# GNN layer on one core: node stage in pairs of blocks, and the output weights scaled by GpSimd

## The reference, cut to what matters

```
h   = relu(layernorm(x))                       # per node
l   = (h @ W_l1) * a                           # per node: the table
w   = relu(edge_basis @ W_fc1) @ W_fc2         # per edge, 192 weights
m   = products of w, l[src] and edge_attr      # per edge
s   = segment_sum(m, dst)                      # per node
out = x + h @ W_si + 0.5 * (s @ W_l2) * a      # per node
```

## Time and profile before

| | us |
|---|---|
| three runs, median (lowest to highest) | 2140.87 (2136.94 to 2141.41) |
| the profiled execution | 2140.02 |
| its span in the profile | 2138.2 |
| busy: PE, DVE, ACT, POOL | 2017.2, 1701.0, 345.4, 1570.7 |
| first gather starts | 89.44 |
| last gather starts | 2118.7 |

### The profile page before, as it was taken

How to read it: one execution, slowest core, us unless ns; L and a number is a source line. 1 busy time by engine, 2 the same in 40 slices (tenths; PEclk the granted TensorE clock), 3 DMA queues, 4 the chain that set the end, 5 groups by cost and what they waited for, 6 DMA issues and landing times.

```text
span 2138.2 us, 42050 instructions
## 1 busy us (share of the span) xinstructions
PE 2017.2 (94%) x11466; PEld 1594.1 (75%) x11466; DVE 1701.0 (80%) x4661; ACT 345.4 (16%) x657; POOL 1570.7 (73%) x1631
## 2 busy tenths in 40 slices
PE   4899999999999999999999999999999999999998
PEld 4677777777777777777777777777777777777776
DVE  7578888878887788788888887888887788888886
ACT  3411111111111111111111111111111111111111
POOL 5277777777777777777777777777777777777775
PEclk9789999999998999999999999999999899998998
DMA  4222322232232233222233232223222222232223
GB/s 123 79 72 69 73 72 70 70 73 71 71 72 69 70 72 72 70 72 71 71 102 73 70 72 71 72 70 73 72 70 72 70 70 71 71 72 70 72 71 91
DMA packets 159932, 158.29 MB, mean 74 GB/s; under 512 B 86882, under 2 KB 131846, under 8 KB 159914
## 3 DMA queue, kind: packets, MB, share of 16 engines
q0 software_dynamic: 77376, 132.16, 24.9%
q1 hardware_dynamic: 81400, 24.49, 5.1%
q10 hardware_dynamic: 1138, 1.43, 0.2%
HBM read 149.90 MB, written 8.03 MB: 74 GB/s over the span
## 4 chain that ended last, share of the span: by engine, by line
POOL 35%; issue 26%; DMA 18%; DVE 15%; PE 4%; POOLq 1%; ACT 0%; DVEq 0%; ACTq 0%; SPq 0%
POOL y L353 35%; DMA y<-table,idx 17%; DVE hot L648 5%; DVE msg L624 5%; DVE dot L618 3%; PE ps_s L850 1%; DVE wself L552 1%; PE ps_s L852 1%; PE ps_w L822 1%; DVE dots L614 1%; DMA table<-y 0%; PE ps_h L815 0%; POOLq L361 0%; PE ps_w L785 0%; DVE stats L508 0%
## 5 line engine op out<-in xcount | busy, mean ns | idle before, releaser
L353 POOL DMA_INDIRECT y<-table,idx x1612 | 1540.0, 955 | 544.1 <-issue 499.4
L822 PEld LDWEIGHTS ps_w<-w_fc,hr 100*128 100x128 f32 x3224 | 539.5, 198 | 331.7 <-issue 331.7
L822 PE MATMUL ps_w<-w_fc,hr 100*128 100x192 f32 x3224 | 663.2, 351 | 0.0
L850 PE MATMUL ps_s<-hot,msg 128*128 128x128 f32 x3224 | 486.3, 298 | 62.2 <-DVE msg L634 61.5
L850 PEld LDWEIGHTS ps_s<-hot,msg 128*128 128x128 f32 x3224 | 437.3, 207 | 107.9 <-DVE msg L634 106.0
L447 ACT ACTIVATE hr<-ps_h 100x512 f32<-100x512 f32 x403 | 240.6, 597 | 1676.8 <-PE ps_h L815 1676.8
L815 PE MATMUL ps_h<-rad,w_fc 10*100 10x512 f32 x806 | 464.3, 657 | 4.9 <-DMA rad<-in_radial 4.9
L614 DVE TENSOR_TENSOR dots<-y,attr_sb 128x384 f32<-128x384 f32 x403 | 225.3, 559 | 280.0 <-DMA y<-table,idx 279.5
L852 PE MATMUL ps_s<-hot,msg 128*128 128x64 f32 x3224 | 432.0, 281 | 0.0
L852 PEld LDWEIGHTS ps_s<-hot,msg 128*128 128x128 f32 x3224 | 423.3, 205 | 0.0
L676 DVE TENSOR_TENSOR acc<-acc,ps_s 64x32 f32 (+1 forms) x1612 | 324.8, 201 | 72.1 <-PE ps_s L852 32.2
(11 more groups left out here) (79 smaller groups left out, 520.4 us busy)
## 6 DMA issues: line engine op xcount, KB each, us to landing
y<-table,idx POOLq DMA_INDIRECT x1612
rad<-in_radial SPq DMA_DIRECT2D x202, 40.0 KB
xres<-in_x SPq DMA_DIRECT2D x7, 560.0 KB, 4.0
table<-y SPq DMA_DIRECT2D x6, 560.0 KB, 3.2
out<-xres SPq DMA_DIRECT2D x6, 560.0 KB, 4.7
idx<-in_src SPq DMA_DIRECT2D x202, 4.0 KB
attr_sb<-in_attr SPq DMA_DIRECT2D x202, 16.0 KB
dst_i<-in_dst ACTq DMA_DIRECT2D x1, 808.0 KB, 6.0
```

The source lines that it names most:

```text
L353: nc.gpsimd.indirect_dma_start(out=y[:, j, t, :], out_offset=None, in_=table, in_offset=bass.IndirectOffsetOnAxis(ap=idx[:, j // HALF, col ...
L822: ins = nc.tensor.matmul(ps_w[:, s, t, 0:NW], hr[:, s, t * P:(t + 1) * P], w_fc2[:, :], start=True, stop=True)
L850: nc.tensor.matmul(ps_s[:, s, 0:4 * W], msg[:, s, t, 0:P], hot[:, s, t, 1:V, :], start=(t == 0), stop=(t == T - 1))
```

## The change

The blocks of a chunk are grouped in four units: blocks 0-1, 2-3, 4-5 and block 6. Per unit there is one copy on ScalarE (512 columns for a pair), one take on VectorE, and one semaphore step each for turning, product and take. The take becomes a `tensor_tensor` of PSUM columns with the attribute broadcast along them, where it was a `tensor_scalar` with a per-partition scalar. The six in-place weight scalings leave VectorE's queue; GpSimd does them ahead of its memset, each waiting for the one before. The side work of VectorE is attached to units 2 of chunk 0 and 0 to 3 of chunk 1. `hid_t` has two places of two blocks each.

```diff
@@ -18,8 +18,9 @@
-LAST_STORES = [(0, 4), (4, CHUNK)]
-TURNED = [0, 1, 0, 1, 0, 1, 2]
+UNITS = [(0, 2), (2, 4), (4, 6), (6, CHUNK)]
+NU = len(UNITS)
+assert NU % 2 == 0
...
@@ -102,7 +103,7 @@
-        hid_t = sb("hid_t", [P, max(TURNED) + 1, 2 * P])
+        hid_t = sb("hid_t", [P, 2, 2, 2 * P])
...
@@ -242,8 +244,8 @@
-            for n, (lo, hi) in enumerate(LAST_STORES):
-                store_table(CHUNKS - 1, CHUNKS - 1 + n, (CHUNKS - 1) % 2, lo, hi)
+            for n, units in enumerate((2, NU)):
+                store_table(CHUNKS - 1, CHUNKS - 1 + n, (CHUNKS - 1) % 2, UNITS[units - 2][0], UNITS[units - 1][1], units)
...
@@ -338,6 +340,12 @@
+            pool.wait_ge(ld_w, 80)
+            for n, (part, scale) in enumerate(((wself[:, 0:MUL0], MUL0 ** -0.5), (wself[:, MUL0:P], MUL1 ** -0.5),
+                                               (wselfz[:, :], MUL1 ** -0.5), (w_out[:, 0:3, :], K_SUM),
+                                               (w_out[0:3 * MUL1, 3, :], K_SUM), (w_out[3 * MUL1:P, 3, :], K_SUM * K_DOT))):
+                nc.gpsimd.tensor_scalar(part, part, float(scale), None, ALU.mult).then_inc(w_end_scaled, 1)
+                pool.wait_ge(w_end_scaled, n + 1)
...
@@ -415,26 +423,30 @@
-                def move(b):
-                    act.wait_ge(tr_done, c * CHUNK + b + 1)
-                    nc.scalar.activation(hid_t[:, TURNED[b], :], ps_h[:, b % 2, 0:2 * P], ACT.Copy).then_inc(hidt_done, 1)
-                for b in range(CHUNK):
-                    if b < CHUNK - 1:
-                        normalize(c * CHUNK + b + 1, b + 1)
+                def move(u):
+                    lo, hi = UNITS[u]
+                    act.wait_ge(tr_done, c * NU + u + 1)
+                    nc.scalar.activation(hid_t[:, u % 2, 0:hi - lo, :], ps_h[:, u % 2, 0:(hi - lo) * 2 * P].rearrange("p (b k) -> p b k", k=2 * P),
+                                         ACT.Copy).then_inc(hidt_done, 1)
+                for u in range(NU):
+                    if u < NU - 1:
+                        for b in range(*UNITS[u + 1]):
+                            normalize(c * CHUNK + b, b)
                     elif not last:
                         act.wait_ge(norm_done, c + 2)
-                        normalize(c * CHUNK + CHUNK, 0)
-                    move(b)
-                    if b == 3 and not last:
+                        for b in range(*UNITS[0]):
+                            normalize((c + 1) * CHUNK + b, b)
+                    move(u)
+                    if u == 1 and not last:
                         deviation(c + 1)
             nc.scalar.activation(early[:, :], eps[:, :], ACT.Sqrt)
             deviation(0)
             act.wait_ge(norm_done, 1)
-            normalize(0, 0)
+            for b in range(*UNITS[0]):
+                normalize(b, b)
...
@@ -522,13 +534,15 @@
-            def take(c, parity, b, first):
-                if not first and b == 0:
+            def take(c, parity, u, first):
+                if not first and u == 0:
                     dve.wait_ge(table_out, c * 16 - 16)
-                dve.wait_ge(node_mm, c * CHUNK + b + 1)
-                nc.vector.tensor_scalar(l_st[:, parity, b, :], ps_w[:, b % 2, 0, 0:C],
-                                        a_sb[:, bass.ds(c * CHUNK + b, 1)], None, ALU.mult).then_inc(l_done, 1)
+                lo, hi = UNITS[u]
+                dve.wait_ge(node_mm, c * NU + u + 1)
+                nc.vector.tensor_tensor(l_st[:, parity, lo:hi, :], ps_w[:, u % 2, 0:hi - lo, 0:C],
+                                        a_sb[:, bass.ds(c * CHUNK + lo, hi - lo)].unsqueeze(2).to_broadcast([P, hi - lo, C]),
+                                        ALU.mult).then_inc(l_done, 1)
...
@@ -543,13 +557,6 @@
-            def scale_more():
-                dve.wait_ge(ld_w, 80)
-                for part, scale in ((wself[:, 0:MUL0], MUL0 ** -0.5), (wself[:, MUL0:P], MUL1 ** -0.5),
-                                    (wselfz[:, :], MUL1 ** -0.5), (w_out[0:3 * MUL1, 3, :], K_SUM),
-                                    (w_out[:, 0:3, :], K_SUM), (w_out[3 * MUL1:P, 3, :], K_SUM * K_DOT)):
-                    nc.vector.tensor_scalar(part, part, float(scale), None, ALU.mult).then_inc(w_scaled, 1)
...
@@ -580,23 +587,22 @@
-                for b in range(CHUNK):
+                for u in range(NU):
                     if not last:
-                        if b == 0:
+                        if u == 0:
                             statistics(c + 1, range(0, 4))
-                        if b == 1:
+                        if u == 1:
                             statistics(c + 1, range(4, CHUNK))
-                        if b == 2:
                             aggregate(c + 1)
-                        if b == 4:
+                        if u == 2:
                             normalizers(c + 1)
-                    take(c, parity, b, first)
-                    if b in between:
-                        between[b]()
-            chunk(0, 0, True, False, {3: distances, 5: scale_more})
-            chunk(1, 1, True, False, {0: farthest, 2: nearest, 3: lowest, 5: outside})
+                    take(c, parity, u, first)
+                    if u in between:
+                        between[u]()
+            chunk(0, 0, True, False, {2: distances})
+            chunk(1, 1, True, False, {0: farthest, 1: nearest, 2: lowest, 3: outside})
...
@@ -765,35 +771,37 @@
-            def had_bank(b):
-                return b - 2 if b >= 2 else -1 - b
-            def turn(c, b, first=False):
-                pe.wait_ge(hid_done, c * CHUNK + b + 1)
+            def turn(c, u, first=False):
+                lo, hi = UNITS[u]
+                pe.wait_ge(hid_done, c * CHUNK + hi)
                 if not first:
-                    pe.wait_ge(hidt_done, c * CHUNK + had_bank(b) + 1)
-                nc.tensor.transpose(ps_h[:, b % 2, 0:P], hid[:, b, 0:P], ident[:, :])
-                nc.tensor.transpose(ps_h[:, b % 2, P:2 * P], hid[:, b, C - P:C], ident[:, :]).then_inc(tr_done, 1)
+                    pe.wait_ge(hidt_done, c * NU + u - 1)
+                for n, b in enumerate(range(lo, hi)):
+                    nc.tensor.transpose(ps_h[:, u % 2, n * 2 * P:n * 2 * P + P], hid[:, b, 0:P], ident[:, :])
+                    ins = nc.tensor.transpose(ps_h[:, u % 2, n * 2 * P + P:(n + 1) * 2 * P], hid[:, b, C - P:C], ident[:, :])
+                ins.then_inc(tr_done, 1)
             def chunk(c, first, last):
-                def linear(b):
-                    pe.wait_ge(hidt_done, c * CHUNK + b + 1)
-                    if b >= 2 or not first:
-                        pe.wait_ge(l_done, c * CHUNK + had_bank(b) + 1)
-                    nc.tensor.matmul(ps_w[:, b % 2, 0, 0:P], hid_t[:, TURNED[b], 0:P], wl[:, :], start=True, stop=True)
-                    nc.tensor.matmul(ps_w[:, b % 2, 0, P:C], hid_t[:, TURNED[b], P:2 * P], wlz[:, :], start=True, stop=True).then_inc(node_mm, 1)
-                for b in range(CHUNK):
-                    if b < CHUNK - 1:
-                        turn(c, b + 1, first and b == 0)
+                def linear(u):
+                    lo, hi = UNITS[u]
+                    pe.wait_ge(hidt_done, c * NU + u + 1)
+                    if u >= 2 or not first:
+                        pe.wait_ge(l_done, c * NU + u - 1)
+                    for n in range(hi - lo):
+                        nc.tensor.matmul(ps_w[:, u % 2, n, 0:P], hid_t[:, u % 2, n, 0:P], wl[:, :], start=True, stop=True)
+                        ins = nc.tensor.matmul(ps_w[:, u % 2, n, P:C], hid_t[:, u % 2, n, P:2 * P], wlz[:, :], start=True, stop=True)
+                    ins.then_inc(node_mm, 1)
+                for u in range(NU):
+                    if u < NU - 1:
+                        turn(c, u + 1, first and u == 0)
                     elif not last:
                         turn(c + 1, 0)
-                    if first and b == 0:
+                    if first and u == 0:
                         pe.wait_ge(w_scaled, 3)
-                    linear(b)
-                    if first and b == 1:
+                    linear(u)
+                    if first and u == 0:
...
@@ -806,7 +814,7 @@
-            pe.wait_ge(w_scaled, 9)
+            pe.wait_ge(w_end_scaled, 6)
```

More of the change, by code:

```diff
@@ L158, in gnn_layer @@
         w_scaled = sem("w_scaled")
+        w_end_scaled = sem("w_end_scaled")
         bn_done = sem("bn_done")
@@ L229, in _, with store_table @@
                 load_x(c, False)
-            def store_table(c, stores, parity, lo, hi):
-                sp.wait_ge(l_done, c * CHUNK + hi)
+            def store_table(c, stores, parity, lo, hi, units=NU):
+                sp.wait_ge(l_done, c * NU + units)
                 sp.sem_inc(sp_passed, 1)
@@ L449, in move_block @@
             def move_block(b, n, bank):
-                act.wait_ge(tr_done, b + (BLOCKS + 1))
-                nc.scalar.activation(hid_t[:, n, :], ps_h[:, bank, 0:2 * P], ACT.Copy).then_inc(hidt_done, 1)
```

(10 more changed lines are left out.)

## The result

The changed kernel's runs have a median of 2134.31 us (2129.95 to 2139.31, 7 runs), the kernel before 2139.85 (2134.9 to 2143.29, 7 runs). The ratio is 0.9975, 95% interval 0.9964 to 0.9986: about 5 us faster, where 11.5 were forecast, and 2134.31 is above the range's end of 2133. The profiled execution took 2139.31 us, the longest of the seven, with a span of 2137.5. So the document compares the stages inside it, and its total only through the seven runs.

What follows compares the result with a forecast made beforehand. GpSimd's gathers were taken to bound the kernel, so only the first gather's start counted. Chunk 2's VectorE queue starting at 38.7 instead of 49.21, plus 1.0 ahead, gave 11.5 us: 2140.02 to 2128.5 us, range 2126 to 2132 (2121 to 2133 with the unheld case).

Steps and rivals of the forecast that it cites:

- What bounds the kernel: Whole run: gathers keep their own pace of 1.26 us, so only an earlier first gather shortens the total.
- Part 1: VectorE's weight scalings in chunk 0: moving them off ends a hold by GpSimd's clear, 15.4 us, plus 0.8 us.
- Part 3: VectorE's `outside` step (L577, L578): its tensor_scalar moves forward into GpSimd's clear and is held 6.2 us, from 32.3 to 38.5.
- rival A: VectorE's small tensor_scalar is not held by the clear: 16.9 us won, 2123.1 us; chance 0.25.
- Rival B: VectorE's new tensor_tensor take in chunk 0 is held by the clear: 6.1 us slower, 2146.1 us; chance 0.04.
- One sign of being wrong: VectorE inside GpSimd's clear: the forecast is wrong if a take there lasts over 1 us.
- Part 2: GpSimd ahead of its clear: the six scalings take 2.6 us, so the clear runs from 17.5 to 38.5 us.
- Part 4: Node-stage chunks on ScalarE, VectorE, TensorE: pairs leave the pace at 6.7 us per chunk, no gain taken, +-2 us overall.
- the sentence on TensorE: TensorE after the new hold: slow level in chunk 2 again as before, no gain or loss, +-1 us.
- the work done ahead during the hold: TensorE and ScalarE while L578 is held: they work ahead by a unit or so, worth about 1 us.
- The handover: From last take's start to first gather (last store, landing, flag, branch): stays at 7.2 us.

Runs made afterwards that it cites:

- single blocks, split: Kernel before, no pairs, with weight scalings on GpSimd ahead of the clear and the two-element tensor_scalar split in two; ratio 0.9923, median 2126.11 us.
- single blocks: Kernel before, no pairs, with only the six weight scalings moved to GpSimd ahead of the clear; ratio 0.9960 against the kernel before.
- with the fill: Changed kernel with the two-element tensor_scalar split in two and ten unused transposes per chunk in TensorE's gap, chunks 1 to 5; ratio 0.9924 against the kernel before.
- The run with the fill and the hold: Changed kernel, two-element tensor_scalar unsplit, plus ten unused transposes per chunk on TensorE in chunks 1 to 5; ratio 0.9979 against the kernel before.
- the kernel without the hold: Changed kernel with the two-element tensor_scalar split into two of one element each, pairs kept; ratio 0.9973 against the kernel before.

## Why the prediction was wrong

*What bounds the kernel* and *Part 1* were right: the hold of 15.4 us was GpSimd's, and without any hold (single blocks, split) the last take comes 14.9 us earlier.

*Part 3*, the step on which the forecast stood against rival A, was right: the two-element tensor_scalar came at 32.51 us (forecast 32.3) and was held until the clear ended. The page of the Trainium skill named there, Vector Engine (DVE) Microarchitecture Reference, section 5.1, has two elements per partition with one source in SBUF in the two-port mode. The trace agrees with it: two elements were held for 7.75 us. Rival B fell: six takes ran inside the clear at their usual length. One sign of being wrong that the prediction named, a take of over 1 us inside the clear, is there (35.88), but as a take that queued behind the held instruction. One reading there was off without effect: between 36.76 and 46.85 us stand six takes of chunk 1, not four or so.

*Part 2* was mis-sized: 4.1 us for the scalings and not 2.6. I took the cast's rate because both have one input; the rate was 2.5 ns, above even the two-input one, and the fixed cost 0.21 us for 0.19. With a start 0.2 us later the clear came 1.7 us late. By the Trainium skill's GPSIMD Engine Reference, section Engine selection, GpSimd is about twice slower for two-input operations, while a one-input operation is roughly at line rate. The rows show 2.5 ns per element for this one-input operation, against 2.2 for the two-input step, so there the page doesn't hold. The move itself paid all the same: with single blocks it brought the first gather from 89.4 to 80.7 us.

*Part 4* is the step that failed: "I get 6.7 us per chunk again", with "I take nothing" for pairs, and the sentence on TensorE behind it, which sees its slow level only in chunk 2: "no gain and no loss, +-1 us". The pace of 6.7 us for pairs is nearly right as long as TensorE is fast (6.95 with the fill). But I took the level from the kernel before, where it stayed up from chunk 3 on. I had laid the three queues side by side for their length and not for their gaps. In each chunk of pairs ScalarE comes to the deviation early, since the aggregate stands behind take 0 and the last three statistics; it waited 3.0 us, and TensorE, which hangs on it for block 6, 1.1 to 1.6. After each such gap of this execution the granted clock read 0.50, and the chunk went on slowly, 8.2 to 9.3 us. From the reciprocal of chunk 3 to that of chunk 6 it took 26.8 us, where it was 19.9 before (54.37 to 74.23) and was forecast to stay: 7.0 us. The run with the fill and the hold parts it. There that stretch took 23.2 us (41.70 to 64.91), so 3.6 us are the falls that the fill takes away. Pairs at full clock cost 1.0 over three chunks (38.51 to 59.35 in the kernel without the hold and with the fill, 20.8 for 19.9), and the remaining 2.4 are the slow chunk right behind the hold. Against it stands a term that I had too small. I gave 1 us for the work done ahead during the hold; the reciprocal of chunk 3, by the forecast due at 54.37 - 11.5 = 42.9 and by the late clear at 44.6, came at 41.8, so that was worth 2.8 us more. The two belong together in part: the chunk done early was followed by one at the slow level.

*The handover* was taken as fixed at 7.2 us and was 9.1: the last take (the second of the row at 76.48) started at 76.9 us, the first gather at 86.0. About 1 us is the last store. SyncE's timeline shows when it was issued:

```profile
30.14 49.41 SPq L239 DMA_DIRECT2D table<-y  x8
```

The issue of the eighth store takes 0.38 us and ends at 79.55, so it begins at 79.17, 1.9 us behind the end of the last take at 77.25. It waits for the landing of the store before it: the two begin 2.42 us apart in both kernels (76.75 and 79.17; before 81.11 and 83.53), and pairs bring the last takes closer to the first of them. Before, the wait was 0.9 us. The other 0.9 us lies between that store and the first gather; what it is was not tried.

The sum: 1.7 (the later clear) - 2.8 (work ahead) + 7.0 (6.0 at the slow clock, 1.0 for pairs at the full one) + 0.3 (from the last reciprocal to the last take, 8.3 for 8.0 us) + 1.9 (handover) = 8.1 us, which is 11.5 less the 3.4 that were won ahead of the first gather. The medians show 5.5 us won, within what the edge stage varies.

## What to carry to other kernels

When an instruction is released from a hold, follow its queue to the next one of the same kind: the holder has only moved, and here it met an instruction of two elements. A step that halves the number of instructions can cost the clock of another engine, if it turns several short waits into one long one (here at most 0.7 us on TensorE with single blocks and a fast clock, 1.1 to 1.8 with pairs). So lay the queues side by side for their gaps too, not only for their length. Where such a gap can't be closed, work without use in it can pay, and has to be tried: in the kernel without the hold the total fell with it, in the one with the hold only the node stage got shorter.

## What the runs showed of the hardware that was not expected

- A float32 tensor_scalar of 128x1 from SBUF to SBUF took 0.14 us in the middle of GpSimd's memset, one of 128x2 was held for 7.75 us; two of 128x1 in its place, 0.14 us each.
- Gaps of 1.1 to 1.6 us on TensorE, in a queue that is otherwise busy, were followed by a granted clock of 0.50 in three chunks of three in the changed kernel; in the kernel without the hold one gap of 1.76 us was not. With ten transposes in the gap it read 1.00 in the chunks that started fast, and fifty of them in all brought the first gather forward by 3.0 us.
- GpSimd's one-input tensor_scalar on float32 costs 2.5 ns per element per partition and 0.21 us fixed (290 ns at 32, 1409 ns at 480 elements); its cast of 1616 elements runs at 0.94 ns per element.
- The same 1612 gathers took between 2028.2 and 2034.8 us from first to last in eleven profiled executions. Why was not found.
